# Cross-attention over 16 sequences: the transfer of the negated maxima issued ahead of the copies of t in its step of the SP queue

## The reference

```python
xn = (input - mu) * rsqrt(var + EPS) * gamma + beta
q  = einsum('oc,ncs->nos', Wq, xn) + bq
kv = einsum('od,nds->nos', Wkv, context) + bkv
att = softmax(einsum('nhqc,nhkc->nhqk', q * scale, k * scale))
y   = einsum('nhqk,nhkc->nhqc', att, v)
out = input + einsum('co,nos->ncs', Wo, y) + bo
```

## Time and profile before

| | |
|---|---|
| time, median of 3 runs | 239.51 us (239.36 to 240.47) |
| time of the profiled execution | 240.03 us |
| span in its profile | 237.1 us |
| granted TensorE clock, mean | 0.935 of full speed |
| busy share: PE, DVE, ACT, POOL | 89%, 85%, 78%, 67% |

### The profile page before, as it was taken

How to read it: one execution, slowest core, us unless ns; L and a number is a source line. 1 busy time by engine, 2 the same in 40 slices (tenths; PEclk the granted TensorE clock), 3 DMA queues, 4 the chain that set the end, 5 groups by cost and what they waited for, 6 DMA issues and landing times.

```text
span 237.1 us, 7252 instructions
## 1 busy us (share of the span) xinstructions
PE 211.0 (89%) x2543; PEld 182.7 (77%) x2543; DVE 200.8 (85%) x585; ACT 184.1 (78%) x373; POOL 157.8 (67%) x153
## 2 busy tenths in 40 slices
PE   6679586999997898999998999999999899999882
PEld 6578564888886787888888888888888788897761
DVE  4578768788898798999997989998999798999765
ACT  2455455699889687998998888988898788888880
POOL 4030424579679676797978967798787678787450
PEclk9956657699999999999999999999999999999996
DMA  5961145245555646666564646666647565543000
GB/s 144 283 249 25 33 112 122 66 113 119 129 131 136 155 103 138 139 143 150 135 155 113 150 112 151 143 141 144 144 105 176 122 150 123 123 96 87 14 2 22
DMA packets 31091, 29.04 MB, mean 123 GB/s; under 512 B 4240, under 2 KB 29840, under 8 KB 31056
## 3 DMA queue, kind: packets, MB, share of 16 engines
q1 hardware_dynamic: 30736, 28.20, 50.6%
q10 hardware_dynamic: 320, 0.40, 0.6%
HBM read 3.80 MB, written 1.05 MB: 20 GB/s over the span
## 4 chain that ended last, share of the span: by engine, by line
PE 65%; DVE 15%; issue 7%; ACT 6%; DMA 4%; POOL 1%; ACTq 1%; DVEq 0%
PE ps_sc L535 11%; PE ps_max L560 10%; PE ps_sc L536 9%; DVE neg_max L886 7%; PE ps_z L494 6%; PE ps_z L496 5%; PE ps_z L495 5%; PE ps_t L510 4%; PE ps_m L601 3%; PE ps_t L511 3%; DVE z_sum L902 3%; DMA wk_sb<-wk 3%; PE ps_m L602 3%; PE ps_m L473 2%; ACT p_full L675 2%
## 5 line engine op out<-in xcount | busy, mean ns | idle before, releaser
L766 POOL TENSOR_TENSOR p_lo<-p_full,p_hi 128x512 f16<-128x512 f32 x122 | 139.9, 1163 | 54.2 <-ACT p_full L675 53.7
L886 DVE TENSOR_REDUCE neg_max<-ps_max 128x2 f32<-128x512 f32 x128 | 85.7, 676 | 11.2 <-PE ps_max L560 10.2
L672 ACT ACTIVATE p_hi<-ps_sc 128x512 f16<-128x512 f32 x128 | 77.3, 604 | 19.1 <-PE ps_sc L536 18.9
L675 ACT ACTIVATE p_full<-ps_sc 128x512 f32<-128x512 f32 x128 | 78.0, 610 | 0.9 <-POOL p_lo L766 0.9
L535 PE MATMUL ps_sc<-t_a,c_seq 128*128 128x256 f32 x256 | 72.8, 305 | 5.5 <-issue 4.4
L536 PE MATMUL ps_sc<-t_b,c_seq 65*128 65x256 f32 x256 | 68.3, 287 | 0.0
L494 PEld LDWEIGHTS ps_z<-u_hi,p_hi 128*128 128x128 f16 x512 | 46.5, 97 | 13.2 <-issue 7.5
L535 PEld LDWEIGHTS ps_sc<-t_a,c_seq 128*128 128x128 f32 x256 | 50.1, 196 | 8.3 <-issue 7.0
L494 PE MATMUL ps_z<-u_hi,p_hi 128*128 128x65 f16 x512 | 53.0, 195 | 3.0 <-DVE p_lo L922 1.8
L495 PE MATMUL ps_z<-u_lo,p_hi 128*128 128x64 f16 x512 | 52.8, 192 | 0.0
L496 PE MATMUL ps_z<-u_hi,p_lo 128*128 128x65 f16 x512 | 52.7, 193 | 0.0
(11 more groups left out here) (107 smaller groups left out, 237.0 us busy)
## 6 DMA issues: line engine op xcount, KB each, us to landing
t_a<-t_a SPq DMA_DIRECT2D x90, 128.0 KB, 2.4
t_b<-t_b SPq DMA_DIRECT2D x30, 128.0 KB, 2.5
c_pad<-c_hi SPq DMA_DIRECT2D x30, 64.0 KB, 2.0
c_seq<-c_hi SPq DMA_DIRECT2D x15, 128.0 KB, 2.4
x_seq<-x_hi SPq DMA_DIRECT2D x15, 128.0 KB, 2.3
x_res<-x_tiles SPq DMA_DIRECT2D x4, 256.0 KB, 6.3
out<-x_res SPq DMA_DIRECT2D x16, 64.0 KB, 2.1
c_seq<-c_lo SPq DMA_DIRECT2D x15, 64.0 KB, 2.1
```

Of the source, the lines that this page charges most:

```text
L672: nc.scalar.activation(p_hi[:, buf, :, :].rearrange("p t s -> p (t s)"), scores, ACT.Exp).then_inc(act_phi, 1)
L675: nc.scalar.activation(p_full[:, head % 2, :], scores, ACT.Exp).then_inc(act_p, 1)
L766: nc.gpsimd.tensor_tensor(p_lo[:, buf, :, :].rearrange("p t s -> p (t s)"), p_full[:, head % 2, :], p_hi[:, buf, :, :].rearrange("p t s -> ...
L886: nc.vector.tensor_reduce(to, ps_max[:, unit % 2, :].rearrange("p (t s) -> p t s", t=KT), X, ALU.max, negate=True).then_inc(dve_max, 1)
```

## The change

In each step of SP's program the block that sends the negated maxima moves from the end of the step to the place just behind UP, ahead of TB, DUP and the output. No DMA, size, engine or semaphore is added or taken away. Where blocks share a step, the order differs; by the tables of the program those are step (0, 2) (TB of sequence 1, then the second part of sequence 0's maxima), step (1, 6) (DUP of sequence 2, then NEG of sequence 2) and the twelve steps (2, 6) to (13, 6) (TB of sequence n+2, then NEG of sequence n+1). NEG of sequences 1 and 15 stands alone in its step.

```diff
-                for turn, m, k in turns_at(TB_FIRST, TB_AHEAD, n, h):
-                    if m > 0:
-                        sp.wait_ge(dve_tlo, turn + 1)
-                        low = packed(t_b_to, m, k)
-                        sp.dma_start(low[0:C, 1], low[C:P, 0]).then_inc(dma_tb[m % 2][k], 16)
-
-                for turn, m, k in turns_at(DUP_FIRST, DUP_AHEAD, n, h):
-                    ...
-                        sp.dma_start(own[C:P], own[0:C]).then_inc(dma_dup[m % 2][k], 16)
-
-                if h == 3 and n >= 2:
-                    ...
-
                 if (e := due(NEG_MAX_FIRST, NEG_MAX_LATER, n, h)) is not None:
                     m, part = max(0, e - 1), e % 2 if e < 2 else 0
                     ...
                         sp.dma_start(t_b_to[C:C + 1, q, :, :].rearrange("o h (t s) -> o (h t) s", t=KT),
                                      rows_from[:, q, :]).then_inc(dma_negmax[q], 16)
+
+                for turn, m, k in turns_at(TB_FIRST, TB_AHEAD, n, h):
+                    ...
+                for turn, m, k in turns_at(DUP_FIRST, DUP_AHEAD, n, h):
+                    ...
+                if h == 3 and n >= 2:
+                    ...
```

More of the change, by code:

```diff
@@ L376, in step @@
                             sp.dma_start(other[to * C:(to + 1) * C], own[C:P]).then_inc(dma_up[m % 2][k], 16)
+                if (e := due(NEG_MAX_FIRST, NEG_MAX_LATER, n, h)) is not None:
+                    m, part = max(0, e - 1), e % 2 if e < 2 else 0
+                    q = m % 2
+                    if m == 0:
+                        sp.wait_ge(act_mt, part + 1)
+                        sp.dma_start(t_b_to[C:C + 1, 0, part * H // 2:(part + 1) * H // 2, :].rearrange("o h (t s) -> o (h t) s", t=KT),
+                                     rows_from[0:HALF_ROWS, part, :]).then_inc(dma_negmax_part[part], 16)
+                    else:
+                        sp.wait_ge(act_mt, m + 2)
+                        for k in range(2):
+                            sp.wait_ge(dma_tb[q][k], 16 * fills(m))
+                        sp.dma_start(t_b_to[C:C + 1, q, :, :].rearrange("o h (t s) -> o (h t) s", t=KT),
+                                     rows_from[:, q, :]).then_inc(dma_negmax[q], 16)
                 for turn, m, k in turns_at(TB_FIRST, TB_AHEAD, n, h):
@@ L395, in step @@
                     sp.dma_start(out[:, m:m + 1, :], x_res[:, m:m + 1, :]).then_inc(dma_out[m % 2], 16)
[L397 to L409, removed]
             run(step)
```

## The result

The changed kernel takes 236.91 us, the median of 16 runs (235.12 to 240.03), beside 241.34 for 16 runs of the kernel before on the same chips (238.25 to 243.26). The ratio is 0.9869, 95% interval 0.983 to 0.9909: 1.3% faster, or 3.1 us of the 239.51 (2.2 to 4.1). The ratio compares the faster executions of both kernels alone, as some of each are slower, so it is nearer to 1 than the two medians make it. Forecast were 4.0 us and 235.5, with a range of 234.0 to 237.9; by the ratio the 239.51 become 236.4. In the wider set of runs the three that the prediction started from lie low.

What follows compares the result with a forecast made beforehand. The prediction took TensorE (PE) as the bound, waiting for NEG: 3.24 us from five short waits plus 0.72 from the long one made 4.0 off 240.03, 236.0, and 235.5 for the median, range 234.0 to 237.9.

Steps and rivals of the forecast that it cites:

- The waits are NEG's, and a wait costs its idle time plus 0.17.: Before the first score product of six sequences, PE waits for NEG; with 0.17 us each for PE's pipeline, 5.4 us together.
- A wait removed comes through whole.: PE is the bound, so a removed wait shortens the kernel fully as long as VectorE, at 94%, keeps up.
- The early steps and what stands behind NEG cost nothing.: Steps (0, 2) and (1, 6) and transfers behind NEG move about 0.7 us later, within their cover: cost nothing.
- NEG can start in TB's place.: In the twelve steady steps ScalarE's eviction ends before TB's issue, so NEG gains 0.7 us or more where PE waits.
- So I take all five as closed: 3.24 us.: The five short waits, at sequences 4, 8, 10, 12 and 13, vanish: 3.24 us, with ends of 0.85 and 3.6.
- I take 0.72, the same transfer's own time in the same traffic.: Sequence 3's long wait of 2.17 us shrinks by 0.72, with NEG issued at 73.75 and still taking 3.0 to land.
- The rival that TB held NEG at sequence 3: TB caused the long landing, so NEG ahead of it lands in 1.9 everywhere; gain 5.1 to 5.4 us, 234.3; chance 0.21.
- The rival that NEG inherits the delay of the place: NEG in TB's queue place takes over TB's delay; gain 1.0 us if whole, about 2.2 if half; chance 0.19.

Runs made afterwards that it cites:

- e6: The kernel before with NEG moved ahead of TB only in the two early steps, (0, 2) and (1, 6); ratio 1.0028 to the kernel before.
- e1: The changed kernel run again without any edit, for a second profile; ratio 0.9859 to the kernel before.
- e7: The changed kernel with UP and DUP one step later and behind NEG, but TB ahead of NEG again; ratio 0.9898, median 236.68 us.
- e2: The changed kernel with 64 already satisfied waits added at the start of TensorE's program; ratio 0.9786 to the kernel before.
- e12: The changed kernel without TensorE's 16 warm-up products (64 instructions fewer); no ratio given, 144.12 us from sequence 3's maxima transpose to sequence 15's.
- e14: The kernel before without TensorE's 16 warm-up products; no ratio given, 146.69 us from sequence 3's maxima transpose to sequence 15's.
- e15: The changed kernel with UP and DUP one step later and behind NEG, and without the warm-up products; ratio 0.9784 to the kernel before.

## Why the prediction was right or wrong

- *The waits are NEG's, and a wait costs its idle time plus 0.17.* Right; the table closes on it.
- *A wait removed comes through whole.* Right: VectorE, at 94%, did not take it over. From 71 us on PE's waits for its maxima are 0.9 us before and 0.5 after, and for GpSimd's low parts 0.8 in both.
- *The early steps and what stands behind NEG cost nothing.* Right (e6), and PE waits for no context or x transfer that it did not wait for before.
- *NEG can start in TB's place.* Right: at sequences 4, 8 and 13 it starts within 0.03 us of the eviction's end.
- *"So I take all five as closed: 3.24 us."* This step failed. 4, 10 and 13 closed, 4 and 13 with nothing to spare; 8 lost 0.64 and now loses 0.53, and 12 lost 0.84 and now loses 1.68, so 1.0 us came of the 3.24. The prediction saw that something held the TB in that place and put it at 0.8 on top of 1.9. It did not ask what it was or what else stands in its way. It is the instruction packet, and UP, DUP and NEG meet it as TB did: NEG's landing at 4, 8 and 13 was 3.0, 3.3 and 3.0 instead of 1.9, and an UP at 12 took the place of the held TB.
- *"I take 0.72, the same transfer's own time in the same traffic."* Failed: 2.17 became 2.20. A landing time was carried along with the issue, as if it ran from there. Here the landing stood still, at 6.2 us after the transpose: one of NEG's 16 packets could start only as the instruction packet ended.
- *The rival that TB held NEG at sequence 3* falls: ahead of TB, NEG took 3.7. By the Trainium skill's rule in "DMA: Bandwidth & Descriptors", section "Queues, rings and completion order", an increment waits for earlier writes of its engine; DUP and UP remained ahead, so the rule is not refuted, only the reading that TB was the one.
- *The rival that NEG inherits the delay of the place* was right about the landings at 3, 4, 8 and 13, and its gain of 1.0 us, if the delay is whole, is what the two first profiles show.

In the two first profiles the waits went from 5.4 to 4.4 us with the 0.17, 1.0 instead of 4.0. That the time came out inside the range all the same is luck. The measured gain is 3.1 most likely because the profile of before, with 4.39, was a lucky one. Two further profiles of the old steady order had 6.84 and 6.96, with the 0.17 8.2 and 8.2. The mean of the three is 7.25; less the 4.4 of the changed kernel's first profile that is 2.8, near the 3.1, and less the mean of its two (e1 has 5.5) 2.3; so few profiles make this an estimate. So the forecast took back too large a share (4.0 of 5.4) of too small a loss. What stays open is why the packets fall at somewhat different places from one execution to the next, and what part of e7's ratio its profile doesn't show.

## What to carry to other kernels

Before a transfer is moved in a queue, ask of each late one whether its issue was late or its landing, and whether the landing moves with the issue: a landing that stands at one place of the work belongs to something else. Then look at all that goes ahead of it, not only at the neighbour: the small transfer that an engine waits for belongs ahead of every large one that has steps of slack, which here was worth 2.7 to 3.0%, against 1.3% for passing one copy. And one profile can be a lucky one: sum a loss from several where it hangs on chance.

## What the runs showed of the hardware

Fetching instructions is not free for others. The page of the changed kernel counts 20 packets and 0.33 MB in q8 for TensorE's 2543 products and as many weight loads. They are TensorE's own: near sequence 3 a packet begins 3.8 to 4.3 us after the transpose in all ten profiles with an unchanged number of TensorE's instructions, 1.1 after it with 64 more (e2), and 6.3 to 6.6 after it with 64 fewer (e12, e14, e15); with 32 fewer it is 4.1, and with 160 more 2.2 and 1.1, which their number alone doesn't explain. The Trainium skill, "Runtime: NRT & Kernel Launch", section "Instruction fetch mechanics", says that instructions are fetched in blocks of 16 KiB by DMA while the engine runs and that the cost is mostly hidden. The size agrees. The cost is not hidden here: a transfer of 8 KB that TensorE waited for landed in 3.0 to 3.7 us instead of 1.8, since one of its 16 packets had to wait for the instruction packet to end.

A granted clock in the profile can be a gap in its record. The window 12 to 24 us (us, busy us of PE, its weight loads, DVE, ACT and POOL, then the clock, the DMA share and GB/s) of the changed kernel and of e12:

```profile
12.00:24.00 12.00, 9.27 (x94) 8.76 (x94) 9.80 (x25) 7.20 (x15) 2.47 (x4) 0.72 0.37 124
```

```profile
12.00:24.00 12.00, 9.93 (x92) 9.40 (x93) 10.38 (x27) 6.64 (x12) 2.03 (x3) 1.00 0.34 113
```

By these rows e12, with fewer warm-up products, was granted 1.00 (2.4 GHz) where the changed kernel had a mean of 0.72. But the same form of product tells another story. In the changed kernel (first row, at a granted clock of 0.50, the 1.2 GHz level) it takes 0.41 us, in e12 at the same point of the work 0.41 as well (second row), and in e12 a little later 0.28 (third row):

```profile
18.59 0.41 PE L511 MATMUL ps_t<-x_seq,a_lo 128*128 128x256 f32 x1
```

```profile
19.51 0.41 PE L511 MATMUL ps_t<-x_seq,a_lo 128*128 128x256 f32 x1
...
23.93 0.28 PE L511 MATMUL ps_sc<-x_seq,a_lo 128*128 128x256 f32 x1
```

So TensorE ran at the lower level there in e12 too. The trace of e12 has no entry for the clock before 23.7 us, and the view counts that as 1.00; the high mean clocks of e12 to e15 (0.96 to 0.98) come from such gaps. The start gained nothing by fewer warm-up products: the transpose of sequence 3 stands at 70.27 and 70.98.
